# Maxima turned on VectorE, stacks with 8 KB rows, and new slots for the first batches, in a two-layer adaLN transformer

## The chip, the cores and the metric

The kernel is one program on one core of one Trainium2 chip. The metric is the device time of one execution in microseconds, from launch to end. The engines of the core run their own instruction streams and wait for each other on semaphores: TensorE (PE, matmul), VectorE (DVE), ScalarE (ACT), GpSimd (POOL), and SyncE (SP), which here does nothing but issue transfers.

## What is computed

Two transformer layers on 8 sequences of 512 tokens with 256 channels. Each layer is an attention block and a feed-forward block, both modulated by a condition vector (adaLN):

```python
mod = (_silu(L0_c) @ L0_wmod).reshape(L0_c.shape[0], 6, 1, -1)
h = _layernorm(x, axis=-1) * (1 + ca) + sa
x = x + ga * _L0_attn_ref(h, ...)      # 16 heads of 16; rms and rope on q, k; softmax over 512 keys
h = _layernorm(x, axis=-1) * (1 + cb) + sb
x = x + gb * _L0_ffn_ref(h, ...)       # ternary weights, 256 -> 1024 -> 1024 -> 1024 -> 256
# the second layer: 16 heads of 16 with biases and a norm per head, then eight experts
```

Both attention blocks compute, for each sequence and head, `softmax(q k^T * scale) v` with 512 queries and 512 keys.

## The kernel before

There are four phases, one behind the other: attention of layer 0 (`A0_`, 0 to 600 us), its feed-forward block (`B_`), attention of layer 1 (`A1_`, from 1282 us) and the experts (`D_`, from about 1820 us). The change is in `attention`, which makes both attention phases; the other two phases stay as they are.

**Slots.** `attention` is written by slots. Each engine's stream is a loop `for p in range(BEGIN, END)`, and what stands in slot p is looked up in tables of numbers: `AT0` and `AT1` for any batch of layer 0 and of layer 1 (32 slots a batch, slot 0 being the first of batch 0), `EARLY0` and `EARLY1` with slots of their own for the first batches, counted from -140. A batch is one sequence, a group (`G`) is four heads, eight slots. In slot p PE makes the scores of one pair of heads and 128 keys (`scores`, L1045), and ACT takes their exponential (`exponential`, L587). `values` (L1064) multiplies by V in f32.

**The maxima.** The softmax needs, for each query, the largest score. PE makes the scores a second time in plain form (`raw`, L1028, one matmul of 512 columns for 128 queries of one head), `AHEAD` = 28 matmuls ahead of the slot, that is 14 slots, two in each slot. DVE reduces each to 128 maxima (`maximum`, L824). PE and DVE share two PSUM banks here (`SM`): `raw` number n waits for `max_s`, the reduction n - 2. After 16 of them a group is complete. Then the job `MT` (slot 8G - 5) lets PE transpose the 128 x 4 maxima of each token tile through the bank `X` (L964), ACT copies `X` to the tile `MTs` one slot on (L596), and SP, two slots after the job, issues two transfers (L356) that put the rows into row 48 of the stacked queries `QS`. `scores` of slot 8G waits for them on `row_ld`. So the maximum is subtracted by the matmul of the scores itself.

**Jobs.** Everything else that PE does for a batch is a job in a slot: `T0`, `T1` (transposes of the normalized input), `QK0` to `QK3` and `V0`, `V1` (projections), `H0` to `H3` (layer 0: transposes of q and k), `YT`, `P` (output). A shared job writes the one bank `X` and waits until the job before it has been copied out of `X`; the first batch's jobs and some others have banks of their own (`OWN_BANK`).

**Stacks.** High and low halves of q and k go through DRAM: `store_features` (L332) writes four tiles of 256 KB into `qk`, and `load_high` (L343) and `load_low` (L349) read them back as twelve transfers of 128 KB, each into 16 partitions of `KT` or `QS`, in an order of rows that the heads need. The high loads wait for both high stores, the low loads for both low ones. `raw` of a batch waits for all twelve (`qk_ld`).

**Weight parts.** In layer 0 `STAGE_AT` also spreads 32 parts of the feed-forward weights over the slots, four a batch: SP loads a part, POOL splits it (L449, L451), SP stores both halves, and DVE reduces one (`f_max`, L891) three slots later.

**DVE's stream** in a slot: division of a finished group, statistics (`STAT`, L868), sums, `f_max`, then `maximum(2p + AHEAD)`, `maximum(2p + AHEAD + 1)`, then copies for jobs.

Of the kernel before, what the change touches and what calls it, by code (L numbers as in the profile page):

```python
# [109 lines left out]
AHEAD = 28  # L110


def placed(base, table):
# [27 lines left out]
OWN_BANK = {("T0", 0): "X", ("T1", 0): "AV", ("V0", 0): "SM0", ("V1", 0): "SM1"} | {(f"QK{i}", 0): f"ST{i}" for i in range(4)}
OWN_BANK0 = OWN_BANK | {(f"QK{i}", 1): f"ST{i}" for i in range(4)} | {(f"H{i}", 0): ("X", "AV", "SM0", "SM1")[i] for i in range(4)}
STAGE_AT = [PAIRS * (i // 4) + (20, 22, 25, 27)[i % 4] for i in range(4 * B)]


def attention(nc, layer, d, keep):
# [13 lines left out]
    jobs |= {8 * G - 5: ("MT", G) for G in range(B * NG)}  # L160
    assert len(jobs) == B * len(names) + B * NG
# [13 lines left out]
    with ExitStack() as ctx:  # L175
# [27 lines left out]
        M = [sb(f"M{k}", [128, TT, HG], F16) for k in range(2)]  # L203
        MTs = [sb(f"MT{k}", [HG, T], F16) for k in range(2)]
# [19 lines left out]
        X16 = X[:, :].bitcast(F16)  # L224
# [15 lines left out]
        job_done, job_out = sem("job_done"), sem("job_out")  # L240
        early_done, early_out, turned_done, turned_out = (sem(n) for n in ("early_done", "early_out", "turned_done", "turned_out"))
# [54 lines left out]
        def _(sp):  # L296
# [126 lines left out]
        def _(pool):  # L423
# [88 lines left out]
            for p in range(BEGIN, END):  # L512
# [56 lines left out]
        def _(act):  # L569
# [20 lines left out]
            def out_of_bank(name, n):  # L590

                if name == "MT":
                    act.wait_ge(*done(name, n))
                    if n >= 2:
                        act.wait_ge(row_ld[n % 2], 32 * (n // 2))
                    nc.scalar.activation(MTs[n % 2][:, :], X16[0:HG, 0:T], ACT.Copy).then_inc(out(name, n)[0], 1)  # L596
                elif name in ("T0", "T1"):
# [123 lines left out]
        def _(dve):  # L721
# [92 lines left out]
            def maximum(n):  # L814
# [28 lines left out]
            for p in range(BEGIN, END):  # L843
# [49 lines left out]
                maximum(2 * p + AHEAD)  # L893
                maximum(2 * p + AHEAD + 1)
# [33 lines left out]
        def _(pe):  # L928
# [8 lines left out]
            def job(name, n):  # L937
# [23 lines left out]
                if name == "MT":  # L961
# [3 lines left out]
                elif name in ("T0", "T1"):  # L965
# [65 lines left out]
            def scores(S, a):  # L1031
# [1054 lines left out]
```

## Time and profile before

| | us |
|---|---|
| median of 3 runs | 2195.03 (2191.36 to 2197.32) |
| the profiled execution | 2191.5 |
| its span, first to last instruction | 2189.8 |
| layer 0: first `raw` on PE | 82.56 |
| layer 0: first scores on PE | 109.51 |
| layer 0: last exponential | 583.6 |
| layer 1: first `raw` on PE | 1327.03 |
| layer 1: first scores on PE | 1357.02 |
| layer 1: last exponential | 1812.8 |

Busy time by engine: PE 1880.9 us (86% of the span), DVE 1350.6 (62%), ACT 1211.6 (55%), POOL 576.3 (26%). These shares run over four phases with different limits, so they say little about this change; the rows below are of single stretches of the two attention phases. A busy PE is not PE at its peak: a matmul of 512 columns in f16 is shown with some 380 ns, while the next begins 215 ns after it. An idle time in square brackets is that of the engine just before the instruction, with what ended it.

### The profile page before, as it was taken

The page shows a single profiled execution, that of the slowest core. Times are in us where ns is not written, and L with a number is a line of the kernel's source. Part 1 is how long each engine was busy: PE and PEld are TensorE (multiplying, and loading weights), DVE is VectorE, ACT ScalarE, POOL GpSimd, SP SyncE. Part 2 cuts the span into 40 slices and gives each one's busy share as a digit, 9 for nine tenths or more (in the row PEclk, how much of TensorE's full clock was granted, in tenths as well). Part 3 has the DMA queues.
Part 4 walks back from the last instruction along what each step waited for, and adds up shares of the span by engine and source line. Part 5 has one row for each costly group of instructions (what it writes and reads, how often), then busy time and mean ns, then how long its engine had stood idle before and what let it go on. Part 6 is the DMA issues. An engine that isn't in the chain of part 4 may idle for free. (4 is left out here: it accounts for less than half of the span.)

```text
span 2189.8 us, 29709 instructions
## 1 busy us (share of the span) xinstructions
PE 1880.9 (86%) x10573; PEld 767.0 (35%) x10573; DVE 1350.6 (62%) x2591; ACT 1211.6 (55%) x1686; POOL 576.3 (26%) x668
## 2 busy tenths in 40 slices
PE   5789999988759999999999956898889983888897
PEld 3323333222224444444444421232223221444443
DVE  5578888878433553553554424777777873677672
ACT  4377888767623432432432233787778873565563
POOL 4676766642200000000000041111111001343443
PEclk8689999999969999999999975999999996899999
DMA  2343554433260000000000023333333304323210
GB/s 107 69 112 88 122 131 108 121 109 85 73 232 1 20 21 12 10 20 11 10 20 1 10 67 53 59 59 59 69 68 59 59 11 160 116 92 129 89 39 19
DMA packets 111985, 147.90 MB, mean 68 GB/s; under 512 B 11874, under 2 KB 95188, under 8 KB 109780
## 3 DMA queue, kind: packets, MB, share of 16 engines
q1 hardware_dynamic: 111828, 145.77, 25.3%
q8 instruction: 103, 1.69, 0.3%
q14 instruction: 54, 0.44, 0.1%
HBM read 100.34 MB, written 45.14 MB: 66 GB/s over the span
## 5 line engine op out<-in xcount | busy, mean ns | idle before, releaser
L824 DVE TENSOR_REDUCE A_M<-A_SM 128x1 f16<-128x512 f32 x1024 | 652.8, 685 | 179.2 <-PE A_SM L1028 177.1
L587 ACT ACTIVATE A_P<-A_ST 128x1024 f32<-128x1024 f32 x512 | 524.0, 1026 | 152.8 <-PE A_ST L1045 148.2
L1028 PE MATMUL A_SM<-A_KT,A_QS 48*128 48x512 f16 x1024 | 358.3, 404 | 78.4 <-DVE A_M L824 67.8
L1337 PE MATMUL B_PA<-B_Hh,B_wh 128*128 128x512 f16 x1024 | 388.1, 379 | 0.0
L1337 PE MATMUL B_PA<-B_Hl,B_wh 128*128 128x512 f16 x1024 | 388.1, 379 | 0.0
L1241 ACT ACTIVATE B_af<-B_PA,B_sv 128x512 f32<-128x512 f32 x192 | 132.0, 688 | 358.1 <-PE B_PA L1337 358.0
L1045 PE MATMUL A_ST<-A_QS,A_KT 49*128 49x512 f16 x1024 | 304.9, 391 | 0.1
L1064 PE MATMUL A_AV<-A_P,A_V 128*32 128x512 f32 x2048 | 280.0, 610 | 5.6 <-ACT A_P L587 5.0
L1028 PEld LDWEIGHTS A_SM<-A_KT,A_QS 48*128 48x128 f16 x1024 | 81.7, 94 | 461.0 <-DVE A_M L824 403.6
L1302 DVE TENSOR_SCALAR B_Hh<-B_af 128x512 f16<-128x512 f32 x128 | 57.9, 452 | 269.7 <-ACT B_af L1241 269.7
L1197 POOL TENSOR_TENSOR B_hl<-B_hf,B_hh 128x512 f16<-128x512 f32 x16 | 18.5, 1157 | 547.8 <-ACT B_hh L1224 547.8
L1337 PEld LDWEIGHTS B_PA<-B_Hl,B_wh 128*128 128x128 f16 x1024 | 100.2, 98 | 119.3
L1337 PEld LDWEIGHTS B_PA<-B_Hh,B_wh 128*128 128x128 f16 x1024 | 100.2, 98 | 119.2
L1304 DVE SCALAR_TENSOR_TENSOR B_Hl<-B_af,B_Hh 128x512 f16<-128x512 f32 x128 | 88.7, 693 | 4.4
L559 POOL TENSOR_TENSOR A_tr<-A_qkf,A_tr 128x512 f16<-128x512 f32 x32 | 37.0, 1159 | 196.5 <-ACT A_tr L681 196.4
L1296 DVE SCALAR_TENSOR_TENSOR B_uf<-B_PD,B_sv,B_af 128x512 f32<-128x512 f32 x64 | 47.8, 747 | 48.4 <-PE B_PD L1337 24.3
L520 POOL TENSOR_TENSOR A_hl<-A_hf,A_hh 128x512 f16<-128x512 f32 x32 | 36.8, 1158 | 121.0 <-ACT A_hh L665 121.0
L1064 PEld LDWEIGHTS A_AV<-A_P,A_V 128*32 128x32 f32 x2048 | 44.6, 108 | 63.7 <-issue 50.3
L868 DVE BATCH_NORM_STATS2 A_st<-A_xt 128x6 f32<-128x256 f32 x64 | 25.1, 416 | 65.6 <-DMA A_xt<-x_tok 60.0
L1337 PE MATMUL B_PA<-B_hh,B_wh 128*128 128x512 f16 x128 | 51.1, 399 | 14.3 <-issue 14.3
L1045 PEld LDWEIGHTS A_ST<-A_QS,A_KT 49*128 49x128 f16 x1024 | 55.8, 94 | 15.3 <-ACT A_P L587 12.6
L969 PE MATMUL A_X<-id,A_xn 128*128 128x128 f32 x120 | 22.8, 321 | 44.5 <-ACT A_xn L688 29.0
(308 smaller groups left out, 3335.8 us busy)
## 6 DMA issues: line engine op xcount, KB each, us to landing
D_w_st<-in_we_dram SPq DMA_DIRECT2D x16, 1024.0 KB, 4.9
qk<-A_tr SPq DMA_DIRECT2D x62, 256.0 KB, 2.4
A_KT<-qk SPq DMA_DIRECT2D x96, 128.0 KB, 4.7
A_QS<-qk SPq DMA_DIRECT2D x96, 128.0 KB, 5.2
A_w_st<-in_w_ffn_dram SPq DMA_DIRECT2D x32, 352.0 KB, 3.8
w_hi<-A_f_hi SPq DMA_DIRECT2D x32, 176.0 KB, 3.5
w_lo<-A_f_lo SPq DMA_DIRECT2D x32, 176.0 KB, 3.6
B_wl<-w_lo SPq DMA_DIRECT2D x1, 5632.0 KB, 25.1
```

Of the source, the lines that this page charges most:

```text
L520: nc.gpsimd.tensor_tensor(hl[:, f, :], hf[:, f, :], hh[:, f, :], ALU.subtract).then_inc(h_low, 1)
L559: nc.gpsimd.tensor_tensor(tr[2 * (i // 2) + 1][:, i % 2, :], qkf[:, i % 2, :], tr[2 * (i // 2)][:, i % 2, :], ALU.subtract).then_inc(qk_lo ...
L587: nc.scalar.activation(P[:, st, 2 * pair:2 * pair + 2, :], ST[:, u % 2, :, :], ACT.Exp, scale=1.0 / math.sqrt(HD)).then_inc(exp_s, 1)
L824: nc.vector.tensor_reduce(M[G % 2][:, tt, o:o + 1], SM[:, n % 2, :], AX, ALU.max, negate=True).then_inc(max_s, 1)
L1028: nc.tensor.matmul(SM[:, n % 2, :], QS[b % 2][r, 2 * g + pair, tt * 128:tt * 128 + 128], KT[b % 2][r, 2 * g + pair, :], start=True, stop=T ...
L1045: ins = nc.tensor.matmul(ST[:, u % 2, a, :], KT[b % 2][r, pair, o:o + 128], QS[b % 2][r, pair, :], start=True, stop=True)
L1064: ins = nc.tensor.matmul(AV[32 * j:32 * j + 32, :], V[b % 3][:, st, g * HG + j, :], P[:, st, j, :], start=st == 0, stop=st == TT - 1)
L1241: nc.scalar.activation(af[:, s % 3, :], PA[:, s % 4, :], ACT.Silu if s < HM else ACT.Gelu, scale=sv[:, which, m:m + 1]).then_inc(a_out, 1)
L1296: nc.vector.scalar_tensor_tensor(out=uf[:, s % 2, :], in0=PD[:, s % 2, :], scalar=sv[:, 1, s:s + 1], in1=src, op0=ALU.mult, op1=ALU.mult). ...
L1302: nc.vector.tensor_scalar(Hh[w][:, m, :], src, HS, None, ALU.mult).then_inc(high, 1)
L1304: nc.vector.scalar_tensor_tensor(out=Hl[w][:, m, :], in0=src, scalar=HS, in1=Hh[w][:, m, :], op0=ALU.mult, op1=ALU.subtract).then_inc(spli ...
L1337: ins = nc.tensor.matmul(out, a, c, start=start and kt == 0 and n_ == 0, stop=stop and kt == kts[-1] and n_ == len(ops) - 1)
```

## The change

It has five parts.

1. **The row of maxima.** The job `MT`, ACT's copy and the tiles `MTs` go. The 16 columns of maxima of a group are laid into the first 16 of 32 columns of a tile `M`, zeroed once, and DVE transposes it in blocks of 32 x 32 (`turn_maxima`, in slot 8G - 5, between its two maxima). The row is then spread over 32-token pieces in the partitions of `rows`, and SP sends it with 8 transfers of 8 x 64 bytes in slot 8G - 4.
2. **Stacks in DRAM** are `[2, 4, 2, HD, H // 2, T]`: a load reads 16 rows of 8 KB in one piece; a store writes 1 KB pieces in another order.
3. **Slots of the first batches.** Layer 0: `V0`, `V1` of batch 1, and the transposes `T0`, `T1` of batch 2, come earlier, ACT's `HI` copies of batch 1 come behind them, and the third part of the modulation goes ahead of `QK` of batch 1 on PE. Layer 1: batch 1 gets its `T` and `QK` jobs before the first `raw`, in banks of their own, and the statistics of batches 2 and 3 get new slots.
4. **AHEAD** is 26.
5. **Weight parts**: two a batch in batches 0 to 4, then 22 parts, one every three slots, in slots 185 to 248.

```diff
-AHEAD = 28
+AHEAD = 26
 EARLY0 = [...
-                            H0=30, H1=31, H2=32, H3=33, HIGH=(36, 36, 36, 36, 37, 37, 37, 37), LOWS=(38, 38, 38, 38))),
+                            H0=28, H1=29, H2=30, H3=31, HIGH=(34, 34, 34, 34, 34, 34, 34, 34), LOWS=(35, 35, 35, 35))),
...
+          placed(-140, dict(STAT=(12, 12, 12, 12), AGG=13, ROOT=13, XN=(21, 21, 21, 21), T0=23, T1=25, HH=(24, 26), HL=(25, 27),
+                            QK0=28, QK1=29, QK2=30, QK3=31, HIGH=(36, 36, 36, 36, 36, 36, 36, 36), LOWS=(38, 38, 38, 38))),
...
-STAGE_AT = [PAIRS * (i // 4) + (20, 22, 25, 27)[i % 4] for i in range(4 * B)]
+STAGE_AT = [PAIRS * b + o for b in range(B - 3) for o in (21, 25)] + [PAIRS * B - 71 + 3 * i for i in range(22)]
...
-    jobs |= {8 * G - 5: ("MT", G) for G in range(B * NG)}
...
-            return d["qk"][n % 2, which, :, :].rearrange("(p a d) t -> a d p t", a=2, d=HD)[a]
+            return d["qk"][n % 2, which, a, :, :, :]
...
-                sp.dma_start(d["qk"][n % 2, which, :, :].rearrange("(f p) t -> p f t", p=128), tile[:, :, :]
+                sp.dma_start(d["qk"][n % 2, which, :, :, :, :].rearrange("a d (f q) t -> q (a d) f t", f=FT), tile[:, :, :]
...
-                G = group_at(p, -3)
+                G = group_at(p, -4)
                 if G is not None:
-                    sp.wait_ge(*out("MT", G))
+                    sp.wait_ge(row_s, G + 1)
+                    g, k = G % NG, (G // NG) % 2
                     for a in range(2):
-                        sp.dma_start(QS[(G // NG) % 2][BLK * a + QROWS - 1:BLK * a + QROWS, 2 * (G % NG):2 * (G % NG) + 2, :],
-                                     MTs[G % 2][2 * a:2 * a + 2, :]).then_inc(row_ld[G % 2], 16)
+                        row = QS[k][BLK * a + QROWS - 1:BLK * a + QROWS, 2 * g:2 * g + 2, :].rearrange("o p (t x) -> o (p t) x", t=TT)
+                        for i in range(4):
+                            sp.dma_start(row[:, :, 32 * i:32 * i + 32], rows[G % 2][32 * i + 8 * a:32 * i + 8 * a + 8, :]
+                                         ).then_inc(row_ld[G % 2], 16)
...
+            def turn_maxima(G):
+
+                dve.wait_ge(max_s, 16 * (G + 1))
+                if G >= 2:
+                    dve.wait_ge(row_ld[G % 2], 128 * (G // 2))
+                nc.vector.transpose(rows[G % 2][:, :], M[G % 2][:, :]).then_inc(row_s, 1)
...
-                if name == "MT":
-                    pe.wait_ge(max_s, 16 * (n + 1))
-                    for tt in range(TT):
-                        ins = nc.tensor.transpose(X16[0:HG, tt * 128:tt * 128 + 128], M[n % 2][:, tt, :], id16[:, :])
```

**On PE in the middle of layer 0, between the two output jobs `P0` and `P1` of a batch.** `A0_SM` is a `raw`, `A0_ST` the scores, `A0_AV` the values, `A0_X` a job. Before:

```order
L1028 MATMUL A0_SM<-A0_KT1,A0_QS1 128x512
L1045 MATMUL A0_ST<-A0_QS0,A0_KT0 128x512 x2
L1028 MATMUL A0_SM<-A0_KT1,A0_QS1 128x512
L964 MATMUL A0_X<-id16,A0_M1 4x128 x4
L1064 MATMUL A0_AV<-A0_P,A0_V1 32x512 x4
L1028 MATMUL A0_SM<-A0_KT1,A0_QS1 128x512
```

And with the change:

```order
L1039 MATMUL A0_SM<-A0_KT1,A0_QS1 128x512
L1055 MATMUL A0_ST<-A0_QS0,A0_KT0 128x512 x2
L1039 MATMUL A0_SM<-A0_KT1,A0_QS1 128x512
L1074 MATMUL A0_AV<-A0_P,A0_V1 32x512 x4
L1039 MATMUL A0_SM<-A0_KT1,A0_QS1 128x512
```

The four small transposes, which wait for the bank `X`, no longer stand between `raw` and the values.

**On PE at the start of layer 1**, around the first `raw` (`A1_KT0`); the rows with `A1_X` are transposes for batch 1 and its first projection. Before:

```order
L934 MATMUL A1_SM<-A1_wh,A1_hl 128x256
L969 MATMUL A1_X<-id32,A1_xn 128x128 x8
L1028 MATMUL A1_SM<-A1_KT0,A1_QS0 128x512 x6
L934 MATMUL A1_X<-A1_hh,A1_wh 128x512
L934 MATMUL A1_X<-A1_hl,A1_wh 128x512
L934 MATMUL A1_X<-A1_hh,A1_wl 128x512
```

And with the change:

```order
L947 MATMUL A1_ST<-A1_hh,A1_wh 128x512
L947 MATMUL A1_ST<-A1_hl,A1_wh 128x512
L947 MATMUL A1_ST<-A1_hh,A1_wl 128x512
L1039 MATMUL A1_SM<-A1_KT0,A1_QS0 128x512 x27
L1055 MATMUL A1_ST<-A1_QS0,A1_KT0 128x512 x2
L1039 MATMUL A1_SM<-A1_KT0,A1_QS0 128x512 x2
```

The projections of batch 1 moved ahead of the first `raw`, and 27 of these now follow each other.

**On SP at the start of layer 0**, the first batch's stores and the first load; a size is that of the target, outermost count first. Before:

```order
L361 DMA A0_xt<-in_x_tok_dram 128x4x256
L332 DMA qk<-A0_tr0 128x2x512
L332 DMA qk<-A0_tr1 128x2x512
L332 DMA qk<-A0_P 128x2x512 x2
L343 DMA A0_KT0<-qk 16x8x512
```

And with the change:

```order
L368 DMA A0_xt<-in_x_tok_dram 128x4x256
L336 DMA qk<-A0_tr0 4x64x512
L336 DMA qk<-A0_tr1 4x64x512
L368 DMA A0_xt<-in_x_tok_dram 128x4x256
L336 DMA qk<-A0_P 4x64x512 x2
L347 DMA A0_KT0<-qk 16x4096
```

The load of batch 3's tokens moved between the stores; a store's target has an outermost count of 4 in place of 128, and a load is 16 runs of 4096 elements (8 KB) in place of 16 x 8 of 512.

## Rows read from the trace of the kernel before

**Rows 1.** Busy time by stretch: batches 3 and 6 of layer 0, 3 of layer 1.

```profile
core 0: us, PE busy (x) PEld busy (x) DVE busy (x) ACT busy (x) POOL busy (x), PEclk, DMA share, GB/s
297.50:358.80 61.30, 56.16 (x397) 18.99 (x396) 52.58 (x95) 49.62 (x70) 43.28 (x54) 1.00 0.45 109
482.20:537.30 55.10, 46.32 (x317) 12.88 (x317) 47.65 (x81) 38.39 (x44) 11.44 (x10) 1.00 0.45 111
1539.70:1599.40 59.70, 53.44 (x357) 17.41 (x357) 45.79 (x86) 47.68 (x66) 9.45 (x14) 0.97 0.34 63
```

**Rows 2.** DVE's groups in batch 3 of layer 0: busy us, mean ns, idle before.

```profile
L824 DVE TENSOR_REDUCE A_M<-A_SM 128x1 f16<-128x512 f32 x64 | 40.7, 684 | 8.4 <-PE A_SM L1028 8.3
L891 DVE TENSOR_REDUCE A_f_max<-A_f_lo 128x1 f32<-128x704 f16 x4 | 3.5, 874 | 0.0
L841 DVE COPY A_tr<-A_X 128x1024 f16<-128x1024 f16 x5 | 3.4, 676 | 0.0
```

**Rows 3.** DVE's groups in batch 3 of layer 1, same columns.

```profile
L824 DVE TENSOR_REDUCE A_M<-A_SM 128x1 f16<-128x512 f32 x64 | 41.0, 686 | 10.9 <-PE A_SM L1028 10.9
L868 DVE BATCH_NORM_STATS2 A_st<-A_xt 128x6 f32<-128x256 f32 x4 | 1.7, 418 | 2.6 <-DMA A_xt<-x_tok 2.6
L850 DVE RECIPROCAL A_rden<-A_AV 128x16 f32<-128x16 f32 x4 | 1.0, 256 | 0.2 <-PE A_AV L1102 0.2
```

**Rows 4.** PE, then DVE, in time order around one MT, layer 0: start, us.

```profile
334.08 0.33 PE L964 MATMUL A_X<-id,A_M 128*4 128x128 f16 x3 [1.82 <-DVE A_xT L832]
...
335.68 1.29 DVE L824 TENSOR_REDUCE A_M<-A_SM 128x1 f16<-128x512 f32 x2 [1.65 <-PE A_SM L1028]
337.62 1.29 DVE L824 TENSOR_REDUCE A_M<-A_SM 128x1 f16<-128x512 f32 x2 [0.65 <-PE A_SM L1028]
```

**Rows 5.** The same around one MT of layer 1.

```profile
1551.40 1.18 SPq L356 DMA_DIRECT2D A_QS<-A_MT  x2
1553.79 1.29 DVE L824 TENSOR_REDUCE A_M<-A_SM 128x1 f16<-128x512 f32 x2 [1.37 <-PE A_SM L1028]
```

**Rows 6.** Start of layer 0 in time order: SP, then PE.

```profile
58.03 0.96 SPq L332 DMA_DIRECT2D qk<-A_tr  x2
60.99 0.33 SPq L343 DMA_DIRECT2D A_KT<-qk  x1
67.49 0.43 SPq L349 DMA_DIRECT2D A_QS<-qk  x1
...
47.40 1.12 PE L969 MATMUL A_X<-id,A_xn 128*128 128x128 f32 x4 [12.00 <-ACT A_hf L605]
...
56.66 0.61 PE L1000 MATMUL A_X<-id,A_qkh 128*128 128x128 f16 x8
...
58.74 6.28 PE L1076 MATMUL A_AV<-A_cs,A_P 128*128 128x8 f32 x48
...
75.04 0.40 PE L934 MATMUL A_X<-A_wh,A_hh 128*128 128x256 f16 x1 [7.44 <-ACT A_V L631]
...
82.56 0.61 PE L1028 MATMUL A_SM<-A_KT,A_QS 48*128 48x512 f16 x2
```

**Rows 7.** Start of layer 1 in time order: SP, then PE.

```profile
1304.98 6.05 SPq L332 DMA_DIRECT2D qk<-A_tr  x4
1311.58 0.34 SPq L343 DMA_DIRECT2D A_KT<-qk  x1
...
1327.03 0.61 PE L1028 MATMUL A_SM<-A_KT,A_QS 48*128 48x512 f16 x2 [7.90 <-DMA A_QS<-qk]
...
1357.02 0.93 PE L1045 MATMUL A_ST<-A_QS,A_KT 49*128 49x512 f16 x2
```

**Rows 8.** Transfers by kind: count, KB each, median us from issue to landing.

```profile
qk<-A_tr SPq DMA_DIRECT2D x62, 256.0 KB, 2.4
A_KT<-qk SPq DMA_DIRECT2D x96, 128.0 KB, 4.7
A_b<-A_bl SPq DMA_DIRECT2D x1, 0.5 KB, 1.6
```

**Rows 9.** SP: issue times (ns, min/median/max) and three pairs in layer 1.

```profile
L356 SPq DMA_DIRECT2D A_QS<-A_MT x128: 558/564/760, 100.9 to 1800.8; - x128
...
1445.30 28.33 SPq L356 DMA_DIRECT2D A_QS<-A_MT  x6
```

More of the change, by code:

```diff
@@ L141 @@
+          dict(STAT=(13, 14, 16, 17), AGG=(18,), ROOT=(19,))]
+MOD_AT = (-138, -134, -120)
+MOD_PE = (-138, -134, -118)
 OWN_BANK = {("T0", 0): "X", ("T1", 0): "AV", ("V0", 0): "SM0", ("V1", 0): "SM1"} | {(f"QK{i}", 0): f"ST{i}" for i in range(4)}
-OWN_BANK0 = OWN_BANK | {(f"QK{i}", 1): f"ST{i}" for i in range(4)} | {(f"H{i}", 0): ("X", "AV", "SM0", "SM1")[i] for i in range(4)}
-STAGE_AT = [PAIRS * (i // 4) + (20, 22, 25, 27)[i % 4] for i in range(4 * B)]
+OWN_BANK |= {(f"QK{i}", 1): f"ST{i}" for i in range(4)}
@@ L146, in attention @@
+OWN_BANK0 = OWN_BANK | {(f"H{i}", 0): ("X", "AV", "SM0", "SM1")[i] for i in range(4)}
+STAGE_AT = [PAIRS * b + o for b in range(B - 3) for o in (21, 25)] + [PAIRS * B - 71 + 3 * i for i in range(22)]
 def attention(nc, layer, d, keep):
@@ L159, in attention @@
     jobs = {slots_of(name, n)[0]: (name, n) for name in names for n in range(B)}
-    jobs |= {8 * G - 5: ("MT", G) for G in range(B * NG)}
-    assert len(jobs) == B * len(names) + B * NG
+    assert len(jobs) == B * len(names)
     shared = [job for p, job in sorted(jobs.items()) if job not in own]
@@ L202, in attention @@
         QS = [sb(f"QS{k}", [128, H // 2, T], F16) for k in range(2)]
-        M = [sb(f"M{k}", [128, TT, HG], F16) for k in range(2)]
-        MTs = [sb(f"MT{k}", [HG, T], F16) for k in range(2)]
+        M, rows = ([sb(f"{n}{k}", [128, 32], F16) for k in range(2)] for n in ("M", "rows"))
         V = [sb(f"V{k}", [128, TT, H, 32]) for k in range(3)]
@@ L240, in attention @@
         job_done, job_out = sem("job_done"), sem("job_out")
+        m_init, row_s = sem("m_init"), sem("row")
         early_done, early_out, turned_done, turned_out = (sem(n) for n in ("early_done", "early_out", "turned_done", "turned_out"))
@@ L438, in _ @@
                 nc.gpsimd.memset(ones2[:, :], 1.0).then_inc(ones_s, 1)
+            for k in range(2):
+                nc.gpsimd.memset(M[k][:, :], 0.0).then_inc(m_init, 1)
             pool.wait_ge(const, 2 if L0 else 1)
@@ L520, in _ @@
                         nc.gpsimd.tensor_tensor(hl[:, f, :], hf[:, f, :], hh[:, f, :], ALU.subtract).then_inc(h_low, 1)
-                if p == slots_of("HL", 0)[1] + 1:
+                if p == slots_of(*(("HL", 0) if L0 else ("HL", 1)))[1] + 1:
                     initial(1)
@@ L590, in out_of_bank @@
             def out_of_bank(name, n):
-                if name == "MT":
[L593 to L597, printed above, removed]
+                if name in ("T0", "T1"):
                     f = int(name[1])
@@ L820, in maximum @@
                 if t == 0 and G >= 2:
-                    dve.wait_ge(*done("MT", G - 2))
+                    dve.wait_ge(row_s, G - 1)
+                if t == 0 and G < 2:
+                    dve.wait_ge(m_init, G + 1)
                 dve.wait_ge(raw_mm, n + 1)
-                o = 2 * a + pair
-                nc.vector.tensor_reduce(M[G % 2][:, tt, o:o + 1], SM[:, n % 2, :], AX, ALU.max, negate=True).then_inc(max_s, 1)
+                o = 8 * a + TT * pair + tt
+                nc.vector.tensor_reduce(M[G % 2][:, o:o + 1], SM[:, n % 2, :], AX, ALU.max, negate=True).then_inc(max_s, 1)
+            def turn_maxima(G):
[3 more added lines that the diff above has]
+                nc.vector.transpose(rows[G % 2][:, :], M[G % 2][:, :]).then_inc(row_s, 1)
             def out_of_bank(name, n):
@@ L893, in _ @@
                 maximum(2 * p + AHEAD)
+                G = group_at(p, -5)
+                if G is not None:
+                    turn_maxima(G)
                 maximum(2 * p + AHEAD + 1)
@@ L1036, in scores @@
                     pe.wait_ge(*out("V1", 0))
-                    if L0:
-                        pe.wait_ge(*out("QK3", 1))
+                    pe.wait_ge(*out("QK3", 1))
                 if u == 0 and a == 1:
-                    pe.wait_ge(row_ld[G % 2], 32 * (G // 2 + 1))
+                    pe.wait_ge(row_ld[G % 2], 128 * (G // 2 + 1))
                 if S >= 2 and a == 1:
@@ L1059, in values @@
                     elif L0:
-                        pe.wait_ge(mod_moved, 3)
+                        pe.wait_ge(*out("H1", 0))
                     else:
@@ L1072, in modulation @@
                 if i == 2:
-                    pe.wait_ge(*out("H1", 0))
+                    pe.wait_ge(*out("T1", 0))
                 for m in range(m0, m1):
@@ L1083, in _ @@
             for p in range(BEGIN, END):
-                if L0 and p in MOD_AT:
-                    modulation(MOD_AT.index(p))
+                if L0 and p in MOD_PE:
+                    modulation(MOD_PE.index(p))
                 raw(2 * p + AHEAD)
```

29 lines of the change are left out of this document (13 added, 16 removed).

## The prediction

> **What bounds the kernel now.** I read the busy times by stretch first, cut by batch. In the middle of layer 0 [rows 1] DVE is busy for 52.6 of 61.3 us; PE shows 56.2, but its rows overlap, so the question is who waits for whom. The grouped rows of the same stretch answer it [rows 2]: 64 maxima of 684 ns wait 8.3 us in all, for `raw` on PE, and hardly anything else of DVE waits. So a batch lasts what DVE's work takes, plus some stops where PE hands out `raw` late. The rows in time order show where [rows 4]: PE waits 1.82 us for bank `X` before three of MT's four transposes, no `raw` goes out meanwhile, and DVE idles 1.65 and 0.65 us. Layer 1 is looser [rows 3]: DVE waits 10.9 us, a shorter piece of it at MT (1.37 us where V0 stands behind MT [rows 5]), and 2.6 us at the statistics, for tokens that SP asked for late. By [rows 1] PE has 53.4 of 59.7 us there.
>
> The two starts come next. In layer 0 [rows 6] the stores are issued from 58.03 us and the last load at 67.49; a load lands 4.7 us behind its issue [rows 8], so by 72.2. `raw` begins only at 82.56, since V1 of batch 1 stands ahead of it on PE and waits 7.44 us for ACT. Earlier still PE idles 12.00 us until ACT has taken T of batch 1 out of `X`; ACT is held by its `HI` copies, which wait for DVE. In layer 1 [rows 7] `raw` truly waits for the loads (7.90 us), and the scores follow at 1357.02.
>
> **Layer 0, start.** ACT takes out T0 and T1 of batch 1 before its last two `HI` copies, so PE's 12.00 us of idle time ends earlier, and the modulation (6.28 us, which stood behind the H jobs) fits into it. 6.3 us of 12 are filled; the rest, 5.5 us, is what QK and H of batch 1 gain: H from 56.66 to about 51.2. Stores and loads move with it. A new wait is H1's for the modulation; it lies behind QK and costs nothing. H2 writes its low parts behind the high store on one queue, for which I put 1 us.
>
> How long a store takes is the open price. Before, 256 KB land 2.4 us after the issue and 0.5 KB after 1.6 [rows 8]: 0.8 us of moving. The store's target now starts with a count of 4 instead of 128. Lower bound: nothing changes, 0.8 us. The nearest row for a target with a small first count is the load, 16 in place of 128: in layer 1 twelve loads of 128 KB take from 1311.58 to 1327.03 [rows 7], less 1.6 us for the last landing 13.9, 1.15 us each, 0.33 us being the issue alone. Per KB that is 2.9 times the store. For a count of 4 I take four times, 3.2 us a store, as the work seems to be divided by the first count; the upper bound is twice that, 6.4. The loads have 8 KB runs; I leave their price at 1.15 (between 0.4, the issue, and 1.15).
>
> The Trainium skill has a rule on this (DMA: Bandwidth & Descriptors, section "Why a DMA increments its semaphore by 16 and not by 1"): a transfer is shared among the largest number of engines, up to 16, that divides the slowest dimension of both sides. For a first count of 4 it would give 4 engines in place of 16, the same factor of four; no row of before has such a transfer.
>
> With H at 51.2, four stores of 3.2 us one behind the other end at about 51.2 + 0.7 + 1.6 + 12.8 = 66.3; the four low loads follow, 4 x 1.15 + 1.6 = 6.2: first `raw` at about 72, where V and T of batches 1 and 2 are no longer late. That is -10.5 against 82.56. One slot less stands between the first `raw` and the scores (AHEAD 26): two maxima, 2 x 0.684 = -1.4; +1 for H2. **Sum -11**; bounds -22 (stores as before, loads 0.4) and -5 (stores 6.4).
>
> **Layer 0, the 32 groups.** MT goes, with PE's wait. [rows 4] is the largest of a batch's four, 2.3 us of idle DVE; over the four, the idle time next to MT that other slots don't have is some 0.85 us each, 3.4 us of a batch's 8.3. DVE gets a transpose of 128 x 32 f16 instead. None is in the trace; the nearest row in size is the RECIPROCAL of 128 x 16 at 256 ns [rows 3], a whole maximum of 684 ns (512 columns) is the upper bound, and 170 ns, a quarter of that, the lower. I take 0.21, somewhat under the RECIPROCAL since the elements are half as wide: 0.85 a batch. Net -2.55 x 8 = -20. Against it stands the new chain of a row: SP issues 8 transfers instead of 2, at 0.56 us each [rows 9]; the last is issued 7 x 0.6 = 4.2 us behind the first and lands 1.6 us later [rows 8], with the transpose and a semaphore about 6.1 us. `scores` of slot 8G stand four slots behind, 7.7 us in layer 0 (61.3 / 32 x 4). Cover of 1.6 us, unless weight or token transfers stand between on SP; for those +0.5 us a batch, +4. **Sum -16**; bounds -25 (no edge, transposes at 0.17 and 1.2 us of idle time at each MT) and +4 (transposes at 0.68, idle time that reappears elsewhere).
>
> **Weight parts.** An `f_max` is 874 ns on DVE [rows 2]. Batches 0 to 4 lose two of four, -1.75 us each; batches 5 to 7 gain 10 in total, +8.7 us. Batch 6 has 47.6 of 55.1 us busy on DVE [rows 1], so it doesn't hide them. **Sum 0**, bounds -3 and +5.
>
> **Layer 1, start.** QK of batch 1 is made before the first `raw`; PE was waiting 7.90 us for the loads, so this is covered. The stores start as before, 1304.98. At 3.2 us each they end at 1304.98 + 1.6 + 12.8 = 1319.4, while the high loads may begin half way, 1313; eight of them end at 1322, four low ones at 1326.8, landed 1328.4, and some 2 us are lost where stores and loads share engines: first `raw` 1330.6, 3.6 later. From there 27 maxima (the order shows 27 `raw` in a row) at 0.684 = 18.5, statistics 4 x 0.42 and what belongs to them 2.2, filling 0.7: scores at 1352. **-5**; bounds -13 (loads 0.4, stores as before) and +3 (stores 6.4). The statistics of batch 3 move to slots 13 to 17 of batch 0, where their tokens are there: one stall of 2.6 us [rows 3] goes, **-3**.
>
> **Layer 1, the 32 groups.** A slot is 1.87 us, four are 7.5; three pairs in [rows 9] are (28.33 - 1.1) / 2 = 13.6 apart for eight slots, so four can be as short as 6.8. The chain of 6.1 has 0.7 to 1.4 us of cover, and where SP stands behind a token load or the output store it has none. MT's idle time is about 0.6 a group (1.37 where V0 is behind, less in the others), transposes cost 0.21 on a DVE that has slack here. I take -1.6 a batch before the chain, -13, and +6 for late rows. **Sum -7**; bounds -20 and +10.
>
> **End.** AHEAD 26 lets the last maxima end one slot closer to the last scores: +1.
>
> **Sum:** -11 - 16 + 0 - 5 - 3 - 7 + 1 = -41. The profiled execution took 2191.5 us, so 2150.5; the median lies 3.5 above it, so **2154.0 us**.
>
> **Rivals.**
> - *Transfers cheaper than taken.* If a store still takes 0.8 us and 8 KB runs make a load 0.5 us, layer 0 gains 9 us more and layer 1 9 us (-20 with the landing of the rows): 2134. For it: a load of 128 KB in 1 KB runs costs more than its bytes, which speaks for run length; against it: the first count of 4.
> - *The groups give nothing.* If DVE's idle time at MT is only where PE's lag shows, and PE's own work (56 of 61 us) sets the pace, it returns at the next job, and the transposes come on top: instead of -23, 0: 2177. For it: PE's high share in both layers.
> - *The chain of the row becomes the bound, slower.* Place: SP, eight issues for each group. Point: the chain must exceed four slots, 7.7 us, that is an issue of (7.9 - 1.6 - 0.3) / 7 = 0.86 us in place of 0.56; the slowest issue of before is 0.76 [rows 9]. At 0.95 us the chain is 7 x 0.95 + 1.9 = 8.6, 0.9 us late in layer 0 and 1.1 to 1.8 in layer 1, for each of 64 groups: +80 in all, 2234. For it: 8 rows of 64 bytes out of eight partitions into one; against: a single row of before is issued in 0.56.
> - *It changes little.* The start is covered by DVE's backlog and MT by PE: about 2190.
>
> **Chances.** Forecast 0.46, cheap transfers 0.24, groups nothing 0.14, chain 0.10, little 0.06. The range takes in the first three with the uncertainty of the store and transpose prices: 2128 to 2180, 0.8 of the chance. What a measurement of this kernel can tell from no change is about 0.3%, 6.6 us: faster is below 2188.4, 0.84; same 0.06; slower, above 2201.6, 0.10.
>
> **What would show it.** In the changed kernel's profile: first `raw` of layer 0 near 72 and first scores near 98.5, `raw` of layer 1 near 1330 less what layer 0 gave; stores landing 4 to 5 us behind their issue; batch 3 of layer 0 at about 59 us with DVE waiting some 5 us in place of 8.4; a transpose of 0.2 us; 8 issues a group of 0.56 us, and no wait of PE for `QS` at the first scores of a group. The forecast is wrong if PE's scores wait for the row's DMA in most groups, if a transpose takes over 0.5 us, or if PE's stops only move to the next job.

## The result and the profile after

The changed kernel takes 2285.67 us (median of 4 runs, 2284.61 to 2291.65) against 2193.2 before on the same chips: 1.0429 times the time, 95% interval 1.0398 to 1.0459. It is slower by 92 us where 41 us less were forecast. Its profiled execution has a span of 2289.9 us (2189.8 before).

Read off the starts of ACT's exponentials, the first and last of each attention phase, the span divides like this (us, profiled executions; the last column is the best kernel of the experiments):

| | before | changed | its stacks undone | four transfers a row, stacks undone, statistics later |
|---|---|---|---|---|
| first exponential, layer 0 | 110.6 | 109.4 | 100.8 | 103.1 |
| exponentials of layer 0 | 473.0 | 485.8 | 462.9 | 454.5 |
| from there to the first of layer 1 | 774.4 | 784.1 | 771.4 | 769.3 |
| exponentials of layer 1 | 454.8 | 533.6 | 481.7 | 425.1 |

79 of the 100 us lie in the attention of layer 1. Batches there (from one batch's first exponential to the next's) take 56, 75.5, 75.4, 75.2, 75.0, 64.6, 63.9 and 48 us; before, 58 to 62 in batches 0 to 4. In layer 0 batches 1 to 4 became shorter, 57 to 58.5 instead of 61 to 63.

The busy times by stretch show both, with the columns of [rows 1]: batch 3 of layer 0, then a stretch of one batch's length in layer 1, from group 1 of batch 3 to group 1 of batch 4, so that it holds both stops whole (batch 3 itself, 1586.2 to 1661.4, has the same clock and busy times within 0.1 us).

```profile
301.10:358.10 57.00, 55.02 (x381) 18.62 (x380) 51.11 (x96) 47.56 (x67) 38.67 (x50) 1.00 0.37 91
1612.20:1687.30 75.10, 55.88 (x341) 17.52 (x340) 46.20 (x91) 46.56 (x61) 9.43 (x15) 0.84 0.25 50
```

Against batch 3 of layer 1 before, DVE's work is what it was (46.2 us against 45.8), PE's is 2.4 us longer at a lower granted clock (0.84 against 0.97), and the rest of the 15 us is waiting. The grouped rows of this stretch, of DVE and then of PE, answer [rows 3]:

```profile
L827 DVE TENSOR_REDUCE A_M<-A_SM 128x1 f16<-128x512 f32 x65 | 42.1, 684 | 18.6 <-PE A_SM L1039 18.4
L878 DVE BATCH_NORM_STATS2 A_st<-A_xt 128x6 f32<-128x256 f32 x4 | 1.7, 420 | 9.2 <-DMA A_xt<-x_tok 9.2
L834 DVE STREAM_TRANSPOSE A_rows<-A_M 128x32 f16<-128x32 f16 x4 | 0.8, 201 | 0.0
...
L1039 PE MATMUL A_SM<-A_KT,A_QS 48*128 48x512 f16 x65 | 23.4, 415 | 11.7 <-DVE A_M L827 11.7
L1055 PE MATMUL A_ST<-A_QS,A_KT 49*128 49x512 f16 x64 | 20.5, 416 | 7.3 <-DMA A_QS<-A_rows 7.3
```

Two stops make the batch long. DVE waits 9.2 us for the next tokens (2.6 before), and the scores on PE wait 7.3 us for their row; each engine then waits for the other. What the two waits grew by, 6.6 and 7.3 us, is 13.9 of the 15.4 us that the stretch is longer. In time order, SP first, then DVE and PE (issues of the row, of the stores, of the tokens):

```profile
1621.35 0.42 SPq L408 DMA_DIRECT2D y<-A_yT  x1
1621.81 5.69 SPq L363 DMA_DIRECT2D A_QS<-A_rows  x8
...
1659.73 1.25 SPq L336 DMA_DIRECT2D qk<-A_tr  x2
1661.03 2.20 SPq L368 DMA_DIRECT2D A_xt<-x_tok  x1
...
1618.54 0.20 DVE L834 STREAM_TRANSPOSE A_rows<-A_M 128x32 f16<-128x32 f16 x1
1670.89 0.43 DVE L878 BATCH_NORM_STATS2 A_st<-A_xt 128x6 f32<-128x256 f32 x1 [9.21 <-DMA A_xt<-x_tok]
...
1632.50 0.61 PE L1055 MATMUL A_ST<-A_QS,A_KT 49*128 49x512 f16 x2 [7.34 <-DMA A_QS<-A_rows]
```

The tokens are issued at 1661.0, right behind two stores, and are there at 1670.9. The row is ready at 1618.7, but SP comes to it only at 1621.8, behind ten loads and the store of `y`, needs 5.7 us for its eight issues, and the last piece is there 5.0 us later, behind the loads' data. Transfers by kind show the same for all batches: tokens took 3.8 us from issue to landing before and 9.9 now.

```profile
A_xt<-x_tok SPq DMA_DIRECT2D x8, 512.0 KB, 9.9
```

And the clock goes down with the stop, so that what follows is slower still. Around the wait for the tokens, with the columns of [rows 1]:

```profile
1655.00:1661.00 6.00, 5.43 (x38) 1.52 (x37) 4.67 (x8) 5.44 (x9) 2.31 (x2) 1.00 0.01 1
1661.00:1667.00 6.00, 1.80 (x12) 0.26 (x10) 0.68 (x2) 2.08 (x3) 0.00 (x0) 0.82 0.45 131
1667.00:1671.00 4.00, 0.00 (x0) 0.00 (x0) 0.11 (x1) 0.00 (x0) 0.00 (x0) 0.50 0.19 65
1671.00:1677.00 6.00, 5.03 (x17) 1.82 (x18) 4.91 (x10) 2.05 (x2) 0.00 (x0) 0.50 0.00 0
1677.00:1687.00 10.00, 10.00 (x68) 3.13 (x65) 7.28 (x19) 7.20 (x10) 2.23 (x3) 0.92 0.03 5
```

The granted clock (third value from the end) is at 0.50, that is 1.2 instead of 2.4 GHz, while PE stands, and stays there for the 6 us after it has begun again.

**What the stores do.** The trace has a record of each packet. Counted in steps of 1 us in one stretch of layer 1, with two stores issued at 1433.6 and 1434.3 and the tokens at 1434.9 (nearly all packets 1 KB):

```
from     packets   engines busy (sum of the packets' time)
1435.0      18      3.8
1436.0      35      3.1
1437.0     109     10.3
1438.0     268     12.7
1439.0     264     11.7
1440.0      87      4.4
1441.0      90      4.4
1442.0      78      4.1
1443.0      62      2.7
```

Before, two such stores ran at 337 packets in one us with 15.4 engines busy. Now only about four engines work for most of the time. The tokens use all 16: for 3 us the others do their part, and then the four that still have stores ahead of them work on to 1445. The tokens landed at 1444.95. So here the rule cited ahead of the result (the Trainium skill, DMA: Bandwidth & Descriptors, section "Why a DMA increments its semaphore by 16 and not by 1": the slowest dimension decides how many engines a transfer gets) agrees with the trace, 4.1 to 4.4 engines for a target that begins with 4. A store of 256 KB then needs 256 / 88 = 2.9 us alone, an estimate from the rows from 1440 on, where the four engines move some 88 KB/us. It fits the tokens: 3.8 us as before and two stores of 2.9 ahead of them make 9.6 us, against 9.9 measured.

Besides, SP itself stands, though hardly in the middle of layer 1 (two stores take 1.25 us to issue there, 0.9 before) and mostly where four stores follow each other. Issue times of the stores by line (ns, smallest, median, largest), of the changed kernel, where before it was 359, 382 and 1753:

```profile
L336 SPq DMA_DIRECT2D qk<-A_tr x62: 504/578/7336, 55.3 to 1813.2; - x62
```

### The profile page after: what moved, and what is told of

The parts are those of the page before. It is cut to its first block and busy times, and to the rows that moved or that the text cites. A ratio compares the mean times of both kernels' runs of the same rounds, so it can differ in the third digit from the quotient of the medians.

```text
span 2289.9 us, 29526 instructions
## 1 busy us (share of the span) xinstructions
PE 1906.2 (83%) x10317; PEld 766.0 (33%) x10317; DVE 1362.0 (59%) x2655; ACT 1185.7 (52%) x1622; POOL 576.5 (25%) x672
## 5 line engine op out<-in xcount | busy, mean ns | idle before, releaser
L827 DVE TENSOR_REDUCE A_M<-A_SM 128x1 f16<-128x512 f32 x1024 | 659.4, 684 | 253.3 <-PE A_SM L1039 248.5
L1039 PE MATMUL A_SM<-A_KT,A_QS 48*128 48x512 f16 x1024 | 377.3, 418 | 126.0 <-DVE A_M L827 98.8
L1055 PE MATMUL A_ST<-A_QS,A_KT 49*128 49x512 f16 x1024 | 315.7, 411 | 64.1 <-DMA A_QS<-A_rows 63.9
L1074 PE MATMUL A_AV<-A_P,A_V 128*32 128x512 f32 x2048 | 293.5, 647 | 2.6 <-ACT A_P L596 2.4
## 6 DMA issues: line engine op xcount, KB each, us to landing
qk<-A_tr SPq DMA_DIRECT2D x62, 256.0 KB
```

Of the source, the lines that this page charges most:

```text
L827: nc.vector.tensor_reduce(M[G % 2][:, o:o + 1], SM[:, n % 2, :], AX, ALU.max, negate=True).then_inc(max_s, 1)
L1039: nc.tensor.matmul(SM[:, n % 2, :], QS[b % 2][r, 2 * g + pair, tt * 128:tt * 128 + 128], KT[b % 2][r, 2 * g + pair, :], start=True, stop=T ...
L1055: ins = nc.tensor.matmul(ST[:, u % 2, a, :], KT[b % 2][r, pair, o:o + 128], QS[b % 2][r, pair, :], start=True, stop=True)
L1074: ins = nc.tensor.matmul(AV[32 * j:32 * j + 32, :], V[b % 3][:, st, g * HG + j, :], P[:, st, j, :], start=st == 0, stop=st == TT - 1)
```

## Experiments

Each ran against the kernel before on the same chip; ratios with 95% intervals.

**The stacks alone undone** (`heads_of`, the store and the buffer as before):

```diff
-            return d["qk"][n % 2, which, a, :, :, :]
+            return d["qk"][n % 2, which, :, :].rearrange("(p a d) t -> a d p t", a=2, d=HD)[a]
...
-                sp.dma_start(d["qk"][n % 2, which, :, :, :, :].rearrange("a d (f q) t -> q (a d) f t", f=FT), tile[:, :, :]
+                sp.dma_start(d["qk"][n % 2, which, :, :].rearrange("(f p) t -> p f t", p=128), tile[:, :, :]
```

> The changed kernel with its part 2 alone undone: stacks in DRAM, their stores (128 x 2 x 512) and their loads (16 x 8 x 512) as before. Theory S (a store whose target begins with a count of 4 keeps 4 of the 16 DMA engines busy for some 3 us, two in a row for 9 to 10 us, and whatever is issued behind it on SP lands late: tokens of the next batch, rows of maxima, the loads): the waits of DVE for A_xt (9.4 us in the middle of layer 1) fall under 3 us, batches of layer 1 go from 75 to about 58 us, the first raw of layer 0 from 82.4 to about 74, batch 0 of layer 0 from 75 to about 62; total 2285.7 to about 2165, between 2150 and 2185. Theory R (the 8 issues of a row in place of 2 block SP, 5.5 us a group, and hold up everything behind them): little changes, 2255 to 2285.

Measured: 2199.35 us, 1.0046 (1.0028 to 1.0065). 86 us are back, so part 2 is the bulk of the loss, but 34 us more than forecast stay: a second cost lies elsewhere. In the middle of layer 1 there are still a wait for tokens and one for a row, in DVE's and PE's rows:

```profile
1458.28 0.43 DVE L878 BATCH_NORM_STATS2 A_st<-A_xt 128x6 f32<-128x256 f32 x1 [3.12 <-DMA A_xt<-x_tok]
...
1491.47 0.61 PE L1055 MATMUL A_ST<-A_QS,A_KT 49*128 49x512 f16 x2 [3.84 <-DMA A_QS<-A_rows]
```

Theory S stands for the larger part, R was not refuted for the smaller. By the table above, the stacks cost 8.6 us in the start of layer 0, 22.9 in its exponentials, 12.7 between the layers and 51.9 in the exponentials of layer 1.

**The stacks alone, added to the kernel before:**

> The kernel before with part 2 alone added: stacks with 8 KB rows, their stores and loads; rows of maxima, tables and AHEAD as before. Theory S: slower than before by most of what the change lost and more, since no other part gives anything back: 2193 to 2260 or 2300, with waits for A_xt of 6 to 10 us a batch in layer 1. Theory R: 2185 to 2200, within 0.3% of before.

Measured: 2281.37 us, 1.0405 (1.0381 to 1.0429), 89 us slower with nothing else changed, and DVE waits 6.0 us for tokens in each of batches 1 to 4 of layer 1 (2.6 to 4.2 before). The stacks cost 86 to 89 us with and without the other parts, so they add to the rest.

**Each store in four of 32 partitions:**

```diff
-                sp.dma_start(...rearrange("a d (f q) t -> q (a d) f t", f=FT), tile[:, :, :]).then_inc(..., 16)
+                to = d["qk"][n % 2, which, :, :, :, :].rearrange("a d (f q) t -> q (a d) f t", f=FT)
+                for q in range(4):
+                    sp.dma_start(to[q, :, :, :], tile[32 * q:32 * q + 32, :, :]).then_inc(..., 16)
```

> The changed kernel with each store of a stack cut into four of 32 partitions, whose targets begin with a count of 32; DRAM layout and loads with 8 KB rows stay. Three issues more for each store, 12 a batch, some 7 us of SP. Theory S: the four parts spread over 16 engines, so the total comes to that of the kernel with the old stacks, within 15 us: 2150 to 2185. Theory R: more issues on SP make it worse, 2290 to 2310. Should it be the 8 KB rows of the loads that cost, or pieces of 1 KB in another order of DRAM, it would stay at 2280.

Measured: 2271.2 us, 1.0359 (1.0329 to 1.0389): a miss, only 14 us come back. The stores themselves are wide again (2.1 us from issue to landing), but the time has moved to SP, as its rows and DVE's around one batch's change show:

```profile
1502.19 5.07 SPq L338 DMA_DIRECT2D qk<-A_tr  x8
1507.31 0.59 SPq L369 DMA_DIRECT2D A_xt<-x_tok  x1
...
1511.44 0.43 DVE L879 BATCH_NORM_STATS2 A_st<-A_xt 128x6 f32<-128x256 f32 x1 [7.28 <-DMA A_xt<-x_tok]
```

Eight issues take 5.1 us, and the tokens stand behind them. What counts is how late the tokens are, not whether the queue or the engines hold them up. This run couldn't tell the width of the stores from the number of issues; the next but one does.

**The maxima back on PE (part 1 undone), the new stacks kept:**

> The changed kernel with its part 1 alone undone: MT on PE, ACT's copy and two issues a group as before; the new stacks, tables and AHEAD 26 stay. AHEAD 26 leaves MT one slot less from the last maxima of a group to the job, so a few us more at MT. Theory S: the stalls stay, and DVE's idle time at MT comes back, 2 to 4 us a batch: 2285 to 2320. Theory R: the stalls behind SP go, 2190 to 2215.

Measured: 2268.84 us, 1.0349 (1.0332 to 1.0366). 17 us less than the changed kernel, so neither theory's number: in layer 0 batches 1 to 4 go from about 57 to 65 us (DVE waits at MT again, now with 26 instead of 28 ahead), in layer 1 from 75 to 68 (six issues a group fewer on SP; that this is the reason was not tested by itself here). Part 1 gives in layer 0 and takes in layer 1.

**Stores wide, loads with 8 KB rows.** The store goes into the same bytes as 128 rows of 2 KB; what the kernel leaves out is the right order of the heads, the work stays the same:

```diff
-                ...rearrange("a d (f q) t -> q (a d) f t", f=FT), tile[:, :, :]
+                ...rearrange("a d (q f) t -> (a d q) f t", f=FT), tile[:, :, :]
```

> The changed kernel with the store of a stack into the same bytes, but taken as 128 x 1024 in one piece of 2 KB each, so that heads come to lie in other places than the loads expect (the values of q and k are mixed up between heads, the work is the same). The loads with their 8 KB rows stay. Theory S (what costs is the first count of 4 of the store's target): as with the old stacks, 2190 to 2205, and the difference to that run is what 8 KB rows in the loads are worth. If the 8 KB rows of the loads delay what stands behind them, 2230 or more.

Measured: 2196.86 us, 1.0019 (1.0002 to 1.0036). One store in one issue, 16 engines, loads unchanged, and all of the stacks' loss is gone. The shape of the store's target is the cause; SP has the same number of issues as in the changed kernel. The pieces are 2 KB here instead of 1 KB, but the stores cut in four kept the 1 KB pieces and their order and landed after 2.1 us, so neither is what costs. The 8 KB rows of the loads are worth 2.5 us against the run with the old stacks, and the two intervals overlap: in layer 1 loads of 128 KB land 1.0 to 1.1 us apart with either kind of row.

**Parts 1 and 2 undone,** the tables, AHEAD 26 and weight parts kept:

> The changed kernel with parts 1 and 2 undone: MT on PE and the stacks of before; what is left is the new tables, AHEAD 26 and the weight parts. By the forecast of before (start of layer 0 -11, of layer 1 -8, groups 0) it would be 2172. By the run with the new stacks and MT (2268.8, 16.8 less than the changed kernel), if both costs add, 2199.4 - 16.8 = 2183. Theory P: 2199 or more. The start of layer 0 should gain about 10 us (first scores at 100.5) in any case, and batches 1 to 5 of layer 0 take 61 to 65 us.

Measured: 2174.04 us, 0.9911 (0.989 to 0.9932). The tables alone gain 19 us, as forecast (2172). Against it the run with the old stacks shows that turning the maxima with eight issues costs 25 us, net. In the profiled executions of the two runs (11.7 us apart only, since that of this run is 8.8 us above its median) the exponentials of layer 0 take 478.7 us without and 462.9 with turned maxima, those of layer 1 453.7 and 481.7: 15.8 us gained in layer 0, 28.0 lost in layer 1.

**Four transfers a row instead of eight,** old stacks. The two head halves of a 32-token piece lie next to each other in `rows`, 16 partitions, and go into the two partitions of `QS` at once:

```diff
-                    for a in range(2):
-                        row = QS[k][BLK * a + QROWS - 1:BLK * a + QROWS, ...].rearrange("o p (t x) -> o (p t) x", t=TT)
-                        for i in range(4):
-                            sp.dma_start(row[:, :, 32 * i:32 * i + 32], rows[G % 2][32 * i + 8 * a:32 * i + 8 * a + 8, :]
+                    row = QS[k][QROWS - 1:BLK + QROWS:BLK, ...].rearrange("o p (t x) -> o (p t) x", t=TT)
+                    for i in range(4):
+                        sp.dma_start(row[:, :, 32 * i:32 * i + 32], rows[G % 2][32 * i:32 * i + 16, :]
```

> The changed kernel with the stacks of before (as in the run with the old stacks, 2199 us) and a row of maxima sent with 4 transfers of 16 x 64 bytes into two partitions instead of 8 of 8 x 64 bytes into one. SP then spends 2.7 us a group on it instead of 5.5. Theory Q (SP's queue is full of issues around slot 31, so that the tokens, due on DVE one slot later, come late; each issue ahead of them counts 0.68 us): the wait for A_xt in layer 1 falls from 3.1 us to about 1, the wait of the scores for the row behind the loads from 3.8 to about 1, batches of layer 1 from 65 to 61 us: 2199 to 2170, between 2160 and 2182. Theory P (what is lost in the run with the old stacks lies in the tables, not on SP): stays within 5 us of 2199.

Measured: 2151.21 us, 0.982 (0.9787 to 0.9852), a gain of 48 us over the run with eight, more than expected. One issue is also cheaper, 496 ns instead of 635. The summary of everything that touches `rows` shows who waited, first with eight transfers, then with four:

```profile
L363 SPq DMA_DIRECT2D A_QS<-A_rows x512: 634/635/1334, 90.0 to 1805.3; - x171
  PE A_ST L1055: 28.0, 11
...
L362 SPq DMA_DIRECT2D A_QS<-A_rows x256: 495/496/686, 93.1 to 1762.9; - x128
  PE A_ST L1053: 0.5, 1
```

28 us of waits of the scores became 0.5. The other 20 are not waits for tokens: these only fell from 3.1 to 2.8 us in the middle of layer 1, against the 1 us expected, and stay the same over the whole layer. What did fall with the stops is the time that the granted clock spent at 0.50 between the first and the last exponential of layer 1, from 86.3 to 47.4 us; how much of the 20 us that makes wasn't tested.

**Statistics of layer 1 later,** in slots 4 to 7, in the changed kernel:

```diff
-AT1 = placed(-48, dict(STAT=(-48, -47, -44, -42), AGG=-41, ROOT=-40, ...
+AT1 = placed(-48, dict(STAT=(-44, -43, -42, -41), AGG=-40, ROOT=-39, ...
```

> The changed kernel with the statistics of layer 1 in slots 4 to 7 of a batch instead of 0, 1, 4 and 6, so four slots (7 us) later than the load of the tokens in slot 31 allows for; stores, rows and all else stay. Theory Q/S (the largest stall of layer 1, 9.4 us a batch at A_xt, is DVE standing in order before tokens that come behind 8 row issues and two narrow stores): batches 1 to 4 of layer 1 lose most of it, 75 to about 67 us, total 2285.7 to about 2255, between 2245 and 2265. If the tokens' wait only hides another one (rows, loads, PE), 2275 to 2286.

Measured: 2238.85 us, 1.0214 (1.019 to 1.0238), 47 us back instead of 30, by moving six numbers. Batches 1 to 4 of layer 1 take 62 to 63 us instead of 75. In the changed kernel the tokens go out in slot 31 and DVE, in order, asks for them in slot 0: the whole delay of SP and of the four engines lands on DVE there. A wait of 2.8 to 3.0 us a batch for the tokens is left.

**Both improvements together, and the weight parts of before on top:**

> The run with the stacks of before and four transfers a row (2151.2 us), with the statistics of layer 1 in slots 4 to 7 as well. There DVE waits 2.8 us a batch for A_xt in batches 1 to 4 (in the middle of layer 1, at slot 0), and group 0 of these batches takes 18 to 20 us against 13 of the others. Theory Q: with the tokens' slack four slots longer the 2.7 us go, some 3 us a batch in four batches: 2151 to 2139, between 2130 and 2145. If V0 and the other jobs of slots 28 to 4 set the length of group 0, not the tokens, 2148 to 2152.

> The same as the run before it, with the weight parts of before (four a batch, slots 20, 22, 25, 27) instead of two a batch and 22 at the end: tells what part 5 of the change is worth. By the forecast it is nothing (0, -3 to +5). By the profiles, batch 6 of layer 0 takes 58.2 us with the new slots and 55.1 before; batches 1 to 4 take 57 with two parts and would take 2 x 0.87 = 1.7 us longer each where DVE sets the pace. Forecast for this run: within 4 us of the run before it.

Measured: 2135.6 us, 0.9742 (0.9725 to 0.976), and with the old weight parts 2137.52, 0.9747 (0.9723 to 0.9772). The first beats both kernels, by 58 and 150 us. Part 5 of the change makes no difference that can be measured: its slots take 1.0 to 1.5 us from each of batches 1 to 4 of layer 0 and give 3.7 back in batch 6. Batches 3 of layers 0 and 1, in the columns of [rows 1]; DVE no longer waits for tokens:

```profile
281.80:338.60 56.80, 55.01 (x381) 18.54 (x380) 51.08 (x97) 47.63 (x66) 38.70 (x50) 1.00 0.42 92
1494.30:1548.40 54.10, 51.23 (x342) 16.52 (x341) 46.06 (x90) 45.71 (x62) 9.43 (x14) 1.00 0.36 69
...
L876 DVE BATCH_NORM_STATS2 A_st<-A_xt 128x6 f32<-128x256 f32 x4 | 1.7, 416 | 0.0
```

## Why the prediction was wrong

The sign was wrong: 2154.0 us forecast, 2285.67 measured. Step by step:

- **The price of a narrow store** was about right: 3.2 us taken, 2.9 estimated from the packets. **Where it was counted** was wrong. The sum has it only in the two starts. But each of 16 batches makes four such stores, and the step that failed is the one on the 32 groups of layer 1, which has only MT, transposes and the row's chain in it and takes no note of the token load right behind the stores on SP. [rows 3] had the warning: DVE already waited 2.6 us a batch for tokens, so that load had no slack, and what delays its data lengthens the wait. In its place stand 9.2 us a batch, and 15 us with the clock and the row's wait: for these 32 groups -7 was forecast, and the exponentials of layer 1 took 78.8 us more, 51.9 of it by the stacks. The same stores cost 22.9 us in layer 0, where the sum has them in no batch either.
- **The row's chain** (0.56 us an issue, cover of 0.7 to 1.4 us, +6 in all in layer 1) was mis-sized, and sized in the wrong place. An issue takes 0.635 us; in most groups the chain does fit into its four slots (PE waited for a row 21 times in 64 groups, 63.9 us in all, 10.4 of it in layer 0). What costs is the group whose row comes behind ten loads, 7.3 us, and again the tokens: the eight issues stand just ahead of stores and tokens, in slot 28. The rival "chain becomes the bound, slower" was named with 0.10 and a price of +80, but for a different mechanism (a chain longer than four slots in every group, above 0.86 us an issue), which didn't occur. With the old stacks eight issues cost 25 us net, four gained 23.
- **Layer 0, groups**: -16 forecast, and 12.8 us more measured for the exponentials of layer 0, since the narrow stores cost 22.9 there, batch 0 above all (74.8 us, 62.6 before: DVE waits 7.8 us for a store and 6.4 for tokens). What the term was about, MT against the turned maxima, was right: -15.8 between the runs with wide stores, with the caution given there. With the parts of the weights where they were before (last experiment), batches 1 to 4 take 57.8 to 58.7 us (61 to 63 before), -3 to -4, no scores of layer 0 wait for a row, and the transposes take 0.20 us (0.21 taken). In the changed kernel DVE's idle time before `maximum` in batch 3 fell from 8.3 us [rows 2] to

```profile
L827 DVE TENSOR_REDUCE A_M<-A_SM 128x1 f16<-128x512 f32 x64 | 40.9, 683 | 5.6 <-PE A_SM L1039 5.4
```

- **Layer 0, start**: -11 forecast, -1.2 measured; -6.6 to -9.8 in the runs with wide stores. H came forward by 2.8 us (to 53.89) and not by 5.5, since the modulation took 10.1 us in its new place instead of 6.28, at a granted clock of 0.50 instead of 0.86 (changed, then before, columns of [rows 1]):

```profile
37.05:47.14 10.09, 10.09 (x49) 10.09 (x49) 9.85 (x15) 2.56 (x4) 6.16 (x4) 0.50 0.11 37
58.74:65.02 6.28, 6.27 (x49) 6.24 (x50) 1.74 (x3) 0.00 (x0) 5.80 (x9) 0.86 1.00 244
```

  So the stores were issued from 55.3 (51.9 in the sum, 58.0 before), a load of tokens lay between them, and their packets ran until about 72 (66.3 in the sum). `raw` began at 82.37 as before, now waiting for the loads:

```profile
82.37 0.61 PE L1039 MATMUL A_SM<-A_KT,A_QS 48*128 48x512 f16 x2 [17.76 <-DMA A_QS<-qk]
```

  The high loads were issued from 65.6, after SP had stood 3.23 us in the issue of the last store. The sum let eight loads run beside the stores, at no cost of their own; by 72 fewer than five of the twelve had moved, and the rest followed at 1.0 to 1.1 us each. One reading was off too: in the kernel before, the last load landed at 74.2, not 72.2, since it is the twelfth in a row and 4.7 us is the median.
- **Layer 1, start**: -5 to -8 forecast. From the last exponential of layer 0 to the first of layer 1 it is +9.7, of which the stacks make 12.7 (771.4 with the old ones, -3). From DVE's first statistics in layer 1 to the first exponential it is 75.3 us against 72.1 before, and 61.4 to 62.9 in the runs with wide stores, so there the new slots, with AHEAD 26, give 9 to 11 us where stores are wide, somewhat more than forecast. The other 6.5 of the 9.7 us lie ahead of it, in the feed-forward block of layer 0, which the change doesn't touch: PE takes 681 us there instead of 675, and so it does (679 to 682) in all runs with the turned maxima, while the three experiments without them have 675 to 676, as before. No run shows why. Nothing in the sum accounted for the stores of batch 1, which now stand before the first row: SP spends 12.92 us in four issues.

```profile
1343.87 12.92 SPq L336 DMA_DIRECT2D qk<-A_tr  x4
...
1378.68 0.61 PE L1055 MATMUL A_ST<-A_QS,A_KT 49*128 49x512 f16 x2 [6.25 <-DMA A_QS<-A_rows]
```

- **Weight parts**: 0 forecast, -2 with the new ones, within the interval.
- **Tables and AHEAD** alone: -19 measured; the forecast's starts and statistics together were -19 (-11, -5, -3). That the sum comes out so well is in part luck: in that run's profiled execution the start of layer 0 gives 7.2 us and the stretch between the layers 8.1, and the exponentials of layer 0 take 5.7 us more.
- **Loads of 8 KB rows**: left at their price; right, the 2.5 us for the kernel can't be told from nothing.
- **The clock** was in no step. It fell to 0.50 in each long stop, so a stop of 9 us costs some more behind it: between the first and the last exponential of layer 1 it was at 0.50 for 145.6 us, before for 33.0, in the best kernel for 15.7. How much of the 15 us a batch is the clock's I haven't separated; with the stops gone, the same stretch has 1.00 and PE's work in it went from 55.9 to 51.2 us.

Not told apart: how the 48 us between eight and four transfers of a row divide between the number of issues and the price of one; and, in the starts, how much of a narrow store's cost is its share of the engines and how much SP's own stand.

## What to carry to other kernels

Where a transfer becomes narrow, look not only at who waits for it but at the next transfer in the queue that uses all engines: it lands when its slowest share lands, behind the narrow one. Then find the load on that queue with the least slack; an existing wait of a few us for it (here the tokens) is the place where a narrow transfer ahead of it is paid in every round of the loop. Giving that load more slack by moving its reader can be worth much: six numbers moved were worth 47 us in the changed kernel, and still 16 us in the one with wide stores and four transfers a row.

## What the runs showed of the hardware

- With stores of 256 KB whose target begins with 4, 4.1 to 4.4 engines were busy and moved some 88 KB/us once the other engines had done their share of the tokens; with 128 the same stores had 15.4 engines busy. Cut into four with a first count of 32 each landed in 2.1 us, but an issue takes 0.6 us.
- Issuing a narrow store could hold SP for up to 7.3 us; before, 1.8 at most.
- The profile gives no landing for the narrow stores ("x62, 256.0 KB" without a time), nor for the rows of maxima. The stores have one in every run in which they are wide, so a missing landing can be a hint of a narrow transfer; for the rows this wasn't tested.
- Rows of 8 KB instead of 1 KB made a load of 128 KB into 16 partitions hardly faster: in layer 1 they land 1.0 to 1.1 us apart with either.
- An issue of 0.5 KB took 0.635 us from 8 partitions into one, and 0.496 us for 1 KB from 16 partitions into two.
- DVE's transpose of 128 x 32 f16 took 0.20 us.
- The same 48 small matmuls of the modulation took 6.28 us at a granted clock of 0.86 and 10.1 us at 0.50.
